# A layer-norm and graph-attention kernel: the queue issues weights, biases and adjacency only after the four first loads of x have landed

## The reference

```
h = relu(layernorm(x))
for each of 2 layers:
    u = h @ h.T / sqrt(384);  a = softmax(u);  delta = a * adj
    attn = delta / (sum(delta) + 1e-10)
    hl, hs, hr = h @ Wl.T + bl, h @ Ws.T + bs, h @ Wr.T + br
    ctx = (attn * upper) @ hl + diag(attn) * hs + (attn * lower) @ hr
    h = relu(layernorm(ctx) * ln_w + ln_b)
out = x + h
```

## Time and profile before

| | |
|---|---|
| median of 3 runs | 1180.22 us (1179.71 to 1180.55) |
| profiled execution, its own time | 1179.74 us |
| its span, first to last instruction | 1178.0 us |
| PE busy | 1167.0 us (99%) |
| DVE, POOL, ACT busy | 939.7, 639.4, 495.0 us |
| mean granted TensorE clock | 0.999 |
| bytes moved | 80.55 MB, 68 GB/s over the span |

### The profile page before, as it was taken

One profiled execution on the slowest core, in us unless ns is written; L12 is line 12 of the kernel. 1 busy time (PEld: TensorE's weight loads), 2 busy tenths in 40 slices (PEclk: granted clock), 3 DMA queues, 4 the chain that ended last, 5 costly groups with the idle time before them and its releaser, 6 DMA issues.

```text
span 1178.0 us, 18565 instructions
## 1 busy us (share of the span) xinstructions
PE 1167.0 (99%) x6998; PEld 1158.1 (98%) x6998; DVE 939.7 (80%) x1872; ACT 495.0 (42%) x1065; POOL 639.4 (54%) x669
## 2 busy tenths in 40 slices
PE   9999999999999999999999999999999999999997
PEld 7999999999999999999999999999999999999997
DVE  6778986689866988769887598876988769875688
ACT  5346433364343543444334443344333454335532
POOL 4685463654635556445555456554475544754347
PEclk9999999999999999999999999999999999999999
DMA  7521312013121131211212112211212113110000
GB/s 245 187 66 55 116 55 81 22 52 117 55 81 37 36 117 55 81 37 62 91 55 81 37 68 85 67 68 37 88 66 81 55 36 113 41 54 1 1 28 27
DMA packets 43481, 80.55 MB, mean 68 GB/s; under 512 B 6912, under 2 KB 24832, under 8 KB 43392
## 3 DMA queue, kind: packets, MB, share of 16 engines
q1 hardware_dynamic: 43104, 78.98, 20.1%
q10 hardware_dynamic: 288, 0.39, 0.1%
HBM read 66.72 MB, written 12.64 MB: 67 GB/s over the span
## 4 chain that ended last, share of the span: by engine, by line
PE 97%; DVE 2%; issue 0%; DMA 0%; ACT 0%; POOL 0%; DVEq 0%
PE rot_ps L344 17%; PE rot_ps L343 17%; PE rot_ps L342 17%; PE u_ps L342 14%; PE u_ps L344 14%; PE u_ps L343 14%; PE rot_ps L405 2%; PE u_ps L398 2%; PE rot_ps L414 1%; DVE xt_sb L670 0%; DMA x_norm<-x_dram 0%; DVE hs L774 0%; DVE z L754 0%; DVE stats L780 0%; DVE x_stats L615 0%
## 5 line engine op out<-in xcount | busy, mean ns | idle before, releaser
L950 POOL TENSOR_TENSOR hw_lo<-proj,hw_hi 128x384 fp32r<-128x384 f32 x256 | 281.6, 1120 | 280.3 <-ACT hw_hi L530 280.3
L342 PE MATMUL rot_ps<-w_hi,ht_hi 128*128 128x384 f32 x1152 | 389.2, 338 | 0.0
L344 PE MATMUL rot_ps<-w_hi,ht_lo 128*128 128x384 f32 x1152 | 385.4, 335 | 0.0
L343 PE MATMUL rot_ps<-w_lo,ht_hi 128*128 128x384 f32 x1152 | 385.2, 334 | 0.0
L343 PEld LDWEIGHTS rot_ps<-w_lo,ht_hi 128*128 128x128 f32 x1152 | 216.5, 188 | 0.0
L342 PEld LDWEIGHTS rot_ps<-w_hi,ht_hi 128*128 128x128 f32 x1152 | 216.5, 188 | 0.0
L344 PEld LDWEIGHTS rot_ps<-w_hi,ht_lo 128*128 128x128 f32 x1152 | 216.2, 188 | 0.0
L505 ACT ACTIVATE u_off<-u_ps 128x128 f32<-128x128 f32 (+1 forms) x128 | 42.5, 332 | 393.7 <-PE u_ps L344 393.5
L717 DVE TENSOR_TENSOR proj<-rot_ps,bias 128x384 f32<-128x384 f32 x256 | 140.1, 550 | 47.4 <-PE rot_ps L344 45.7
L962 POOL TENSOR_TENSOR dg<-et_hi,tri 128x256 fp32r<-128x256 f32 x128 | 113.5, 887 | 94.5 <-PE u_ps L344 94.5
L530 ACT ACTIVATE hw_hi<-proj 128x384 fp32r<-128x384 f32 x256 | 127.9, 520 | 66.0 <-DVE proj L717 66.0
(11 more groups left out here) (89 smaller groups left out, 2038.7 us busy)
## 6 DMA issues: line engine op xcount, KB each, us to landing
out_dram<-z SPq DMA_DIRECT2D x64, 192.0 KB, 1.9
x_norm<-x_dram SPq DMA_DIRECT2D x15, 768.0 KB, 4.3
xt_sb<-x_t_dram SPq DMA_DIRECT2D x15, 768.0 KB, 4.5
adj_a<-adj_t_dram SPq DMA_DIRECT2D x8, 1024.0 KB, 5.4
adj_b<-adj_t_dram SPq DMA_DIRECT2D x8, 1024.0 KB, 5.4
x_norm<-rows_dram SPq DMA_DIRECT2D x15, 512.0 KB, 3.8
x_a<-x_dram SPq DMA_DIRECT2D x8, 768.0 KB, 4.6
x_b<-x_dram SPq DMA_DIRECT2D x8, 768.0 KB, 4.6
```

Source lines behind the costliest of these rows:

```text
L342: pe.matmul(dst, a_hi, b_hi, start=first and m == 0, stop=False)
L343: pe.matmul(dst[:, 0:b_lo.shape[1]], a_hi, b_lo, start=False, stop=False)
L344: done = pe.matmul(dst, a_lo, b_hi, start=False, stop=last and m == n - 1)
L950: pool.tensor_tensor(hw_lo[:, t, n, :], proj[:, t % 2, n, :], hw_hi[:, t, n, 0:dim].bitcast(F32), ALU.subtract).then_inc(hw_lo_done, 1)
```

## The change

SP gets four waits between its own loads of x and the first weight load. They cover all four tiles, also the two that ScalarE's queue loads. Everything that follows in SP's program is issued behind them; nothing is added to or removed from the other engines.

```diff
             for t in range(0, TILES, 2):
                 sp.dma_start(x_norm[:, t, :], rows(x, 0)[:, t, :]).then_inc(x_first[t], 16)
+            for t in range(TILES):
+                sp.wait_ge(x_first[t], 16)
             for c in range(KB):
                 load_w(c)
             load_bias(0)
```

## The result

The changed kernel takes 1182.51 us (median of 15 runs, 1182.0 to 1182.9), the kernel before 1180.22 us (15 runs, 1179.71 to 1181.08). The ratio is 1.0018, with a 95% interval of 1.0011 to 1.0026. The medians differ by 2.3 us: the kernel is slower, by about 0.2%, and the interval doesn't say on which side of 0.2%. The forecast was 1182.4. The profiled execution took 1182.84 us, of which the span is 1181.1, against 1179.74 and 1178.0 before: this one execution shows 3.1 us, more than the median.

A forecast was written before the change was run, and what follows sets the result against it. PE, busy 99% of the span, was taken to bound the kernel. Waits 0, x 0 and restart +2.2 us made span 1180.2; with 1.74 around it 1181.9, plus 0.5 for the median 1182.4 us (+0.19%), range 1180.6 to 1183.2.

The forecast's parts named there:

- The waits themselves cost 0: SyncE's queue: the four waits remove no instruction and no byte; waits and issues count 0.
- Nothing gained from x: Start, x loads to statistics of graph 0: gain 0, bounds 0 to 0.1 us, since VectorE waits only for tile 0.
- The weights: First weight load: issued at 5.1 to 5.3, landing at 8.95, at most 9.5; just in time for ScalarE at 9.32.
- Rival A: First weight load takes 4.2 us or more: shift 2.7 to 3.0, time 1182.9 to 1183.2; chance 0.12.
- The shift: SyncE's queue behind the weights: graph 1's statistics rows land 2.2 us later, at most 2.7, at least 0.3.
- the prediction's own sign: Prediction is wrong if the statistics rows' landing moved by something else than the first weight's landing.
- It reaches PE one for one: VectorE and POOL chain of step 0: the whole 2.2 us arrives at step 1's scores, 50.0 instead of 47.76.
- Rival B: The 10 to 12 us DMA slump isn't repeated in the shifted stream: shift 1.0, time 1181.2; chance 0.18.
- Rival C: Graph 1's slow `ht_lo` comes ahead of POOL's weight split, 2.0 us less, kernel ends at 1180.4; chance 0.06.
- Rivals D and E: D: slack or backlog absorbs the shift, 1180.2 to 1180.5, chance 0.09. E: x lands sooner, faster, chance 0.03.
- the 0.5 us added for the median: Last step of the sum: the kernel before's median lay 0.5 us above its profiled execution, so 1181.9 became 1182.4.
- the chances: Whole kernel: slower by over 0.2% 0.29, faster 0.02, within 0.69; 0.2% is 2.4 us.

The follow-up runs named there:

- second profile: The changed kernel measured and profiled once more, unedited, against the kernel before: 1182.07 us, ratio 1.0018; profiled execution 1182.05 us.

## Why the prediction was right

The time, the sign and the mechanism were right. Point by point:

1. *The waits themselves cost 0*: the same waits behind the weights gave 1.0004, no difference that can be measured.
2. *Nothing gained from x*: the statistics of graph 0 start at 4.07 against 4.19 and the first scores at 11.62 against 11.73; at the bound that I gave.
3. *The weights*: issue at 5.26 (5.1 to 5.3 foretold), 3.9 us to landing (3.85 to 4.2), landing at 9.16, 0.05 us ahead of ScalarE. The fit of the Trainium skill (DMA: Bandwidth & Descriptors, Anatomy of one DMA), 3.35 us as an estimate, is short of the 3.9 us of the trace. The page gives it for loads that GpSimd issues, and this one is issued by SP, which the prediction didn't say; the measurement decides. Rival A's dear restart did not come: 3.9, not 4.2.
4. *The shift*: I took 2.2 us, with 2.7 as its upper bound. The first weight's landing was shifted by 9.16 - 6.79 = 2.4 us, and the statistics by 2.39 in the second profile, which is close to its kernel's median. In the first profile it was 3.26, outside the bound. By the prediction's own sign, that landing moved by something else than the first weight's; what it is stays open. The term fits the second profile, and its spread was set too small. It also took the kernel before for steadier than it is: with the same program up to there, its statistics began at 17.46 in one profile and at 19.02 in another.
5. *It reaches PE one for one*: the table shows it over 3.3 us. Foretold were the first evacuation at 22.1, POOL's centring at 37.7 and the scores of step 1 at 50.0; the second profile has 22.32, 37.80 and 50.00, the first 23.19, 38.63 and 50.82. The idle time of about 2.5 us, "in one piece or with some of it earlier", came out as 0.78, 0.36 and 1.63 us in the first profile.
6. *Rival B* fell: the slump moved along. *Rival C* did not happen, the split still began ahead of the slow low part. But the price on which it rests is real: with the split moved away PE's wait vanished, and the distance from the statistics to the scores fell from 30.15 to 28.32 us, 1.8 us where the rival said 2.0. In the changed kernel the split (46.96, 2.65 us) ended at 49.61 and the slow low part at 50.16, 0.55 us later, which is about what a low part takes alone (1.27 us for two): it hardly got on while the split ran. This agrees with the rule of the Trainium skill (SBUF — State Buffer, Who interferes with whom). *Rivals D and E* fell.

That 1182.4 came within 0.1 us of 1182.51 is luck: the same kernel took 1182.07 in its second measurement, and the 0.5 us added for the median against the profiled execution of the kernel before had no cause behind it; in the changed kernel the profiled execution lies 0.3 us above the median. That the ratio stayed below 1.002 was a matter of tenths of a microsecond, as the chances said.

## What to carry to other kernels

In this kernel a wait in the DMA queue cost nothing while the DMA engines still had work in front of them (1.0004). When they ran dry it cost what they didn't move until the stream was full again, here 2.5 us for a pause of 3.57 us. Look for the price not at the loads that are held back but at the last one in the queue that somebody is waiting for, even if its own issue hasn't moved. And a load that is needed early should not stand behind a larger one that isn't; in a kernel that is bound by one engine, a late start is paid in full as soon as it exceeds the slack of the chain behind it, and here there was next to none.

## What the runs showed of the hardware

- The price of a dry queue: in the changed kernel the DMA engines moved nothing from 5 to 6 us, 134 GB/s in the next and 290 in the one after, before the usual 400; a pause of 3.57 us in the issue delayed the first landing by 2.4 us. In the other kernels with the four waits the rates of the first microsecond after the stop were 120 to 217 GB/s.
- Three loads of 192 KB that each broadcast one row to 128 partitions pull the rate down to 85 to 115 GB/s (the lowest microsecond) towards their end, at 10 us or at 13 us as the stream lies; the same bytes from ordinary rows flow at 350 to 411. Another broadcast, of 512 KB from `rows_dram`, is slow as well: 213 GB/s from 26 to 27 us in the kernel before, when it was under way. The broadcasts of layer 1 follow behind `adj_b`, from about 30 us on, and there the lowest half microsecond was 252 GB/s; why those suffer less is open.
- The ten warm-up matmuls of 128x512 from 1.50 us on took 7.63 us in one profile and 6.36 in another, at the same granted clock of 1.00, and between 5.95 and 7.53 us in the other kernels. It costs nothing here, since PE then waits for x.
- The profile's idle times of PE are shorter than the stops: 0.78, 0.36 and 1.63 us against 0.54 before make 2.2 us, and the scores start 3.06 us later. Ahead of each stop the last matmul is still counted as busy while nothing follows it: matmuls start 0.17 us apart and are counted 0.34 us long. And stops shorter than that show no idle time at all. If the same matmul is compared in both kernels, PE is 0.08 us ahead at 26.7 us and 0.32 us behind at 30.2, without any idle time in the profile; it is 1.34 behind after the stop at 38.8, 1.96 after that at 45.2, and 3.06 at the scores.
